# Two elementwise steps of a convolution moved to GpSimd, and the value matmul of attention in three fp32r passes

## The reference

```python
def attn(inputs, conv_w, conv_b, wq, bq, wk, bk, wv, bv, wo, bo, proj_w, proj_b):
    x = conv(inputs, conv_w, padding='SAME') + conv_b        # (2, 1024, 768)
    q, k, v = split(x, 3, axis=-1)                            # 256 columns each
    # blocks of 128 tokens, 16 heads of 64
    qh, kh, vh = q @ wq + bq, k @ wk + bk, v @ wv + bv
    scores = where(causal, (qh / sqrt(64)) @ kh.T, -1e9)
    p = softmax(scores)
    o = p @ vh                                                # the value step
    return (o @ wo + bo) @ proj_w + proj_b

x = x + attn(layernorm(x), ...)
x = x + ffn(layernorm(x), ...)      # x @ W_base.T + b_base + gated low-rank terms
```

## Time and profile before

| | us |
|---|---|
| median of 3 runs | 956.61 |
| lowest and highest run | 955.38, 957.01 |
| the profiled execution | 955.38 |
| its span, first to last instruction | 953.7 |
| TensorE busy | 869.6 (91%) |
| TensorE weight loads busy | 727.8 (76%) |
| DVE busy | 466.3 (49%) |
| ScalarE busy | 396.7 (42%) |
| POOL busy | 164.8 (17%) |

### The profile page before, as it was taken

One profiled execution on the slowest core, in us unless ns is written; L12 is line 12 of the kernel. 1 busy time (PEld: TensorE's weight loads), 2 busy tenths in 40 slices (PEclk: granted clock), 3 DMA queues, 4 the chain that ended last, 5 costly groups with the idle time before them and its releaser, 6 DMA issues. The chain is left out here.

```text
span 953.7 us, 14958 instructions
## 1 busy us (share of the span) xinstructions
PE 869.6 (91%) x5376; PEld 727.8 (76%) x5376; DVE 466.3 (49%) x1383; ACT 396.7 (42%) x1048; POOL 164.8 (17%) x180
## 2 busy tenths in 40 slices
PE   3899989998999878999999999999822999999997
PEld 3346767747888667888888888888612999999997
DVE  6948776969665334232323333333315444444442
ACT  5601223631322168776767676776304111111100
POOL 2000110000000013434344352523300000000000
PEclk9999999999999989999999999999965899999999
DMA  6235223126322133022212121211246122212211
GB/s 226 78 115 193 74 86 102 37 73 222 109 89 89 68 121 121 3 77 62 106 34 88 33 88 35 89 46 46 89 122 215 45 89 89 64 70 88 89 45 45
DMA packets 41136, 84.85 MB, mean 89 GB/s; under 512 B 9076, under 2 KB 27508, under 8 KB 40309
## 3 DMA queue, kind: packets, MB, share of 16 engines
q1 hardware_dynamic: 38772, 75.69, 24.3%
q0 software_dynamic: 2304, 8.39, 2.2%
HBM read 60.60 MB, written 23.07 MB: 88 GB/s over the span
## 5 line engine op out<-in xcount | busy, mean ns | idle before, releaser
L71 PE MATMUL ffn_yp<-ffn_w_hi,ffn_xT_hi 128*128 128x354 f32 (+1 forms) x384 | 128.2, 334 | 24.2 <-DVE ffn_w_lo L1115 24.2
L73 PE MATMUL ffn_yp<-ffn_w_hi,ffn_xT_lo 128*128 128x354 f32 (+1 forms) x384 | 126.7, 330 | 0.0
L72 PE MATMUL ffn_yp<-ffn_w_lo,ffn_xT_hi 128*128 128x354 f32 (+1 forms) x384 | 126.4, 329 | 0.0
L667 ACT ACTIVATE attn_pr<-attn_pr,attn_negmax 128x128 f32<-128x128 f32 x256 | 99.3, 392 | 10.7 <-DVE attn_negmax L721 9.8
L625 POOL TENSOR_TENSOR attn_pr<-attn_pr,attn_rrec 128x512 f32<-128x512 f32 x64 | 66.7, 1042 | 195.4 <-DVE attn_rrec L716 195.4
L262 ACT ACTIVATE conv_w_hi<-conv_raw 128x1024 fp32r<-128x1024 f32 x36 | 38.1, 1058 | 134.7 <-DVE conv_raw L350 86.2
L71 PEld LDWEIGHTS ffn_yp<-ffn_w_hi,ffn_xT_hi 128*128 128x128 f32 x384 | 74.1, 193 | 26.0 <-issue 16.5
L72 PEld LDWEIGHTS ffn_yp<-ffn_w_lo,ffn_xT_hi 128*128 128x128 f32 x384 | 74.1, 193 | 0.0
L73 PEld LDWEIGHTS ffn_yp<-ffn_w_hi,ffn_xT_lo 128*128 128x128 f32 x384 | 74.0, 193 | 0.0
L72 PE MATMUL attn_qkp<-attn_c_lo,wqk_hi 128*128 128x256 f32 x256 | 73.0, 285 | 0.0
L342 DVE TENSOR_TENSOR conv_w_lo<-conv_raw,conv_w_hi 128x1024 fp32r<-128x1024 f32 x36 | 44.0, 1223 | 52.8 <-ACT conv_w_hi L262 52.8
(11 more groups left out here) (167 smaller groups left out, 2109.4 us busy)
## 6 DMA issues: line engine op xcount, KB each, us to landing
conv_raw<-in_conv_w SPq DMA_DIRECT2D x48, 384.0 KB, 3.5
xn<-in_x SPq DMA_DIRECT2D x16, 512.0 KB, 4.8
attn_stage<-in_x SPq DMA_DIRECT2D x8, 1024.0 KB, 4.8
x_scratch<-attn_stage SPq DMA_DIRECT2D x8, 1024.0 KB, 3.9
...
```

Source lines behind the costliest of these rows:

```text
L71: pe.matmul(out, w_hi, x_hi, start=first, stop=False)
L72: pe.matmul(out, w_hi, x_lo, start=False, stop=False)
L73: return pe.matmul(out, w_lo, x_hi, start=False, stop=last)
L667: e = act.activation(pr[:, j4, un], pr[:, j4, un], ACT.Exp, bias=negmax[:, j2, un:un + 1], scale=-1.0, accum_out=rsum[:, j2, un:un + 1])
```

## The change

In the convolution:

- `mix` moves from DVE to POOL. POOL makes the mixes of pieces 0 and 1 ahead of its loop, and that of `k + 2` at the end of iteration `k`.
- `transform` is split: DVE keeps the instruction for the first two combinations (`outer`), POOL makes the third and fourth (`inner`). Both signal on their own semaphore, and `high_input` and `native_unit` wait for both.
- The powers of the second sequence stand in POOL's loop, each ahead of the mix of its iteration.
- Tile 7 of both sequences is scaled on ScalarE instead of DVE.
- The low inputs of the second sequence come one iteration earlier.

In attention:

- The projected values and the transposed probabilities are split into high (ScalarE) and low parts (DVE); the value step is a three-pass product of 128x256 for each of the two blocks, with both heads' values as weights and both heads' probabilities as columns. Two of the four 64x128 quarters of its result are used.
- `op` grows to a whole bank, and the copies of its halves to `oT_hi` and `oT_lo` become two instructions each.
- Whoever waited for `v_ready` or `pT_ready` now waits for the low part.

```diff
-        DVE_SCALES = (2, 5, LT - 1)
+        DVE_SCALES = (2, 5)
-        LOW_AT = {3: (0, 0), 5: (0, 2), 7: (0, 4), 8: (0, 6), 26: (1, 0), 27: (1, 2), 28: (1, 4), 29: (1, 6)}
+        LOW_AT = {3: (0, 0), 5: (0, 2), 7: (0, 4), 8: (0, 6), 25: (1, 0), 26: (1, 2), 27: (1, 4), 28: (1, 6)}
...
+            def mix(k):
+                r = raw[:, k % RR]
+                pool.wait_ge(raw_loaded[k % RR], 16 * (k // RR + 1))
+                pool.tensor_tensor(r[:, :, 3], r[:, :, 1], r[:, :, 2], ALU.add).then_inc(s["sum_ready"], 1)
+                pool.wait_ge(s["sum_ready"], k + 1)
+                pool.tensor_tensor(r[:, :, 4], r[:, :, 3], r[:, :, 0], ALU.subtract)
+                pool.tensor_tensor(r[:, :, 3], r[:, :, 3], r[:, :, 0], ALU.add).then_inc(s["mix_ready"], 1)
+
+            def inner(n, c):
+                pool.wait_ge(s["xT_ready"], LT if n == 0 else LT + c + 1)
+                pool.tensor_tensor(u[:, c, 2], xT[:, c, 1:L + 1:2], xT[:, c, 2:L + 2:2], ALU.add)
+                pool.tensor_tensor(u[:, c, 3], xT[:, c, 2:L + 2:2], xT[:, c, 1:L + 1:2], ALU.subtract).then_inc(s["u23_ready"], 1)
...
-            for j in range(LT):
-                power(1, j)
+            mix(0)
+            mix(1)
+            for k in range(-1, NK):
+                if k in U_AT:
+                    n, c = U_AT[k]
+                    inner(n, c)
+                    inner(n, c + 1)
+                if k in STATS_AT:
+                    power(1, STATS_AT[k])
+                if 0 <= k < NK - 2:
+                    mix(k + 2)
...
-                dve.tensor_tensor(u[:, c, 0:2], d01, d23, ALU.subtract)
-                dve.tensor_tensor(u[:, c, 2], xT[:, c, 1:L + 1:2], xT[:, c, 2:L + 2:2], ALU.add)
-                dve.tensor_tensor(u[:, c, 3], xT[:, c, 2:L + 2:2], xT[:, c, 1:L + 1:2], ALU.subtract).then_inc(s["u_ready"], 1)
+                dve.tensor_tensor(u[:, c, 0:2], d01, d23, ALU.subtract).then_inc(s["u01_ready"], 1)
...
+                    for h in range(2):
+                        e = slice(h * DH, (h + 1) * DH)
+                        o = act.activation(oT_hi[e, opar, j].rearrange("p (b t) -> p b t", b=GB), op[e, :, h], ACT.Copy)
...
+                if live(J - TR, NJ):
+                    dve.wait_ge(s["pT_hi_ready"], J - TR + 1)
+                    dve.tensor_tensor(pT_lo[:, (i - TR) % 2], ptp[:], pT_hi[:, (i - TR) % 2], ALU.subtract).then_inc(s["pT_lo_ready"], 1)
...
+                    if kind == "v":
+                        dve.wait_ge(s["v_hi_ready"], VT * eg + n + 1)
+                        k, cols = vcols(n)
+                        dve.tensor_tensor(v_lo[:, k, cols], gp[:, bank], v_hi[:, k, cols], ALU.subtract).then_inc(s["v_lo_ready"], 1)
...
-                        for h in range(2):
-                            mm = pe.matmul(op[h * DH:(h + 1) * DH, b], vf[:, b, j * P + h * DH:j * P + (h + 1) * DH],
-                                           pT[:, j2, b, h * P:(h + 1) * P], start=True, stop=True)
+                        mm = three_pass(pe, op[:, b].rearrange("p h t -> p (h t)"), v_hi[:, b, j * P:(j + 1) * P], v_lo[:, b, j * P:(j + 1) * P],
+                                        pT_hi[:, j2, b], pT_lo[:, j2, b], True, True)
```

67 lines of the change are left out of this document (31 added, 36 removed).

## The result

The changed kernel takes 986.81 us (median of four runs, 981.88 to 990.36), the kernel before 956.81 (four runs, 955.38 to 957.78): slower by 3.1%, ratio 1.0311 with a 95% interval of 1.0262 to 1.0362. The forecast was 993.8 in a range of 970 to 1006.

A forecast was written before the change was run, and what follows sets the result against it. TensorE was taken to bound steady attention fully and the convolution nearly, there with 9.5 us of waits for DVE's low weight part. 11.6 - 1.2 + 12.5 + 5 + 10.5 = 38.4 on 955.4 gave 993.8 us, range 970 to 1006.

The forecast's parts named there:

- The sign: Whole kernel: the change makes it slower, chance 0.95; within 0.2% 0.02, faster 0.03.
- the ring (C): Eight convolution iterations with statistics: POOL's mix waits behind its power, rounds of 7.0 us instead of 6.30, +12.5 us.
- R3: Rival: POOL's mix short enough (1.0 us) to leave the eight iterations' ring; 952.7 us, faster by 0.3%, chance 0.03.
- A: Start of the convolution to the fifth weight pair: TensorE waits for transforms and POOL's mixes, +11.6 us.
- The lock: POOL adds and DVE instructions with two SBUF inputs exclude each other, so their durations add; 5.0 us a chunk at the start.
- R1: Rival: POOL and DVE do not block each other at full length; 976.2 us, chance 0.22.
- D: Turn to the second sequence: POOL's queue of inner adds and mix, 10.1 us a pair against 6.87, net +5 us.
- B: First split weights: DVE has one mix less before the third low weight part, -1.2 us.
- R2: Rival: POOL's every-second-element adds cost 2.0 us, or TensorE's clock falls to 1.2 GHz; 1010 us, chance 0.11.
- E: Attention: +7.3 us from the value step over 64 steps, +2.2 in the start-up, +1 in the drain; +10.5 us.
- The value step: Attention, TensorE: six 128x256 matmuls plus 0.09 us, 0.79 us against 0.68, +0.114 for each of 64 steps.
- The last phase: After attention, to the kernel's end: no change, 0 us.

## Why the prediction was right, and where its sizes were off

**The sign and the ring (C) were right.** The order of POOL's queue was the step of the prediction with the largest term: +12.5 forecast, +11.1 measured, a round of 6.82 us for 7.0. The two kernels with fifteen mixes on POOL differ in that order and in nothing else, and by 20.4 us. R3 had this place right too and its condition wrong: I had POOL leave the ring only if its mix took 1.0 us or less. With its 2.2 us it leaves the ring at once when it stands ahead of the power. Its place in the queue decided, and not its duration.

**A was mis-sized: +11.6 for +4.7.** It is nearly the whole distance between 993.8 and 986.8. The lock was as forecast, but an `inner` add takes 1.03 us, not the 1.29 of the line through two contiguous rows, and an `outer` and an `inner` overlap by a quarter of a microsecond, so that a chunk costs 4.0 us and not 5.04. TensorE needs 3.43. I had it start 3.6 us late and then wait for every chunk, 6.7 us in all at the third pair; it started 2.4 us late and waited for none. Its first chunk ran at the lower clock (0.50 from 29.95 to 34.20), slower than the chunks came, so each later chunk was ready before TensorE was. So the excess over TensorE's pace, on which the term rests, was 0.6 us a chunk instead of 1.6 and small enough to be covered: an error of a quarter in the pace became one of almost three times in the excess. From the third pair to the fifth I had 4.9 us, with POOL's queue at mix 4 by 68.3; it was there at 61.4, and TensorE lost 1.8 us in waits for POOL's mixes. R1 falls by these rows: the engines do block each other at full length.

**D, +5 for +3.9,** came out close by errors that cancel, and that is luck. Pair 24 starts at 203.75, 18.6 us late and 1.5 of that new, where I had 5.1, since the adds are cheaper. The later pair lost 4.6 instead of 2.4: 3.0 with a wait of 2.8 for POOL's mix, and 1.6 behind it at the lower clock (0.54 from 229.15 to 232.49), for which I had nothing. The waits behind the turn gave back 2.2 for 2.4. **B, -1.2 for -1.5,** was right.

**Missing: +2.8 behind the eight iterations.** The window ahead of that piece:

```profile
149.30:161.40 12.10, 6.77 (x30) 4.96 (x28) 6.86 (x12) 3.97 (x4) 5.37 (x8) 0.97 0.24 76
```

TensorE was busy 6.77 us of 12.10 and then ran at the lower level for 6 us. I had such a clock in a rival (R2), and in the sum at nothing. But not all of it is the change's. Three kernels with the convolution of before lost 1.6 us at the same place against the profiled execution of before, with a granted clock of 0.72 in the 6 us behind the eight iterations, where that execution had 1.00 and the change 0.50; two kernels that have the ring, the fifteen mixes behind the power and the change with the inner adds on DVE, lost 1.6 us at 0.72 too.

**E, +10.5 for +11.6.** The value step is right in size: 0.80 us for 0.79, and the lateness grows by 6.5 us over the 52 steps from the twelfth scores to the last, 0.125 each against 0.114. One reason in it was wrong: the 0.09 us is not a switch to full precision, since the kernel with the fp32 value step has no gap where fp32 follows fp32r and has the 0.09 between two fp32 products, where the tile changes. That it moved from one side of the value step to the other holds all the same, because the new step has the whole tile. ScalarE's and DVE's additions stayed covered in the steady part, as forecast. At the start of attention the lateness grows by 2.6 us, with the steps' own 0.12 among it, where I had 2.2 on top of them; but kernels with the attention of before lose 0.1 to 3.5 us there, depending on the clock, so this term can't be read to a microsecond. The end was +1 by forecast and +2.4 measured, 1.6 of it from the halves.

**The last phase: 0 for -1.8.** Its code is unchanged. Of the eleven other kernels with the same code there, ten spend 0.2 to 3.4 us less on it than the profiled execution of before, and one as much. It belongs to that execution, not to the change.
